# Six similarities and a transposed state sum inside the scan loop of a two-layer decoder kernel

## What is computed

```python
x = _layernorm(x + _L0_attn_ref(x, ...))                 # 1: gated delta rule
x = _layernorm(x + _L0_xattn_ref(x, ctx_1024, ..., 16))  # 2: strided cross attention
x = _layernorm(x + _L0_ffn_ref(x, ...))                  # 3: feed forward with sines
x = _layernorm(x + _L1_attn_ref(x, ...))                 # 4: selective scan
x = _layernorm(x + _L1_xattn_ref(ctx_1024, x, ...))      # 5: attention, 8 heads
x = _layernorm(x + _L1_ffn_ref(x, ...))                  # 6: token-shift mix
```

```python
# 4
def step(h, inp):
    u_t, dt_t, B_t, C_t = inp
    dA = jnp.exp(dt_t[..., None] * A)
    h = h * dA + (dt_t * u_t)[..., None] * B_t[:, None, :]
    y_t = jnp.einsum('bds,bs->bd', h, C_t) + D_param * u_t
    return (h, y_t)
...
y = y * _silu(z)
return y @ W_out + b_out
# 5 (x is the context here, latents the stream; 8 heads)
xn = _layernorm(x, gamma_media, beta_media)
ln = _layernorm(latents, gamma_lat, beta_lat)
...
attn = jax.nn.softmax(sim, axis=-1)
# 6
r = jax.nn.sigmoid(jnp.einsum('btc,dc->btd', xr, W_r))
...
out = r * jnp.einsum('btc,dc->btd', k_act, W_v)
```

## Time and profile before

| | us |
|---|---|
| median of 3 runs | 406.8 (404.0 to 408.42) |
| the profiled execution, its own time | 406.31 |
| its span in the trace | 403.4 |
| mean granted TensorE clock, share of full | 0.954 |
| scan loop, first to last step | 158.0 to 289.8 |
| units of block 5 behind the loop, last `output5` ends | 389.9 |
| end of the span | 403.4 |

### The profile page before, as it was taken

One profiled execution on the slowest core, in us unless ns is written; L12 is line 12 of the kernel. 1 busy time (PEld: TensorE's weight loads), 2 busy tenths in 40 slices (PEclk: granted clock), 3 DMA queues, 4 the chain that ended last, 5 costly groups with the idle time before them and its releaser, 6 DMA issues. The chain is left out here.

```text
span 403.4 us, 5113 instructions
## 1 busy us (share of the span) xinstructions
PE 331.6 (82%) x1578; PEld 221.6 (55%) x1578; DVE 319.8 (79%) x638; ACT 210.8 (52%) x462; POOL 224.4 (56%) x228
## 2 busy tenths in 40 slices
PE   5538748789788889779997888895899999999991
PEld 2332447787564626332433543352498877898870
DVE  1599999996877798999999899799868544754536
ACT  2642222231255669577777165663456666674650
POOL 3599899993413142779899889995502700100002
PEclk9957959999999989999999999999999999999996
DMA  8900000000000003335444434443200000000001
GB/s 267 382 30 0 0 3 1 2 1 2 0 2 0 0 2 107 95 101 160 143 139 138 150 99 126 122 137 103 61 0 1 2 0 2 1 2 2 0 0 52
DMA packets 11520, 24.52 MB, mean 61 GB/s; under 512 B 1231, under 2 KB 2255, under 8 KB 11239
## 3 DMA queue, kind: packets, MB, share of 16 engines
q1 hardware_dynamic: 11495, 24.22, 19.0%
HBM read 23.63 MB, written 0.59 MB: 60 GB/s over the span
## 5 line engine op out<-in xcount | busy, mean ns | idle before, releaser
L1057 POOL TENSOR_TENSOR arena<-arena 128x512 f32<-128x512 f32 x63 | 79.7, 1278 | 24.7 <-DVE arena L685 23.2
L685 DVE TENSOR_TENSOR_SCAN arena<-arena,ps 128x512 f32<-128x512 f32 x64 | 77.2, 1208 | 0.0
L1736 PE MATMUL ps<-arena,first_in 128*128 128x512 f32 x128 | 66.5, 603 | 5.7 <-POOL arena L1057 5.6
L1349 ACT ACTIVATE arena<-ps,arena 128x248 f32<-128x248 f32 x64 | 29.3, 463 | 41.4 <-DVE arena L716 41.4
L678 DVE TENSOR_TENSOR ps<-arena,ps 128x512 f32<-128x512 f32 x64 | 43.4, 680 | 6.0 <-PE ps L1724 5.4
L1313 ACT ACTIVATE arena<-arena,neg_a 128x508 f32<-128x508 f32 x64 | 43.2, 709 | 9.5 <-DVE arena L685 8.6
L1103 POOL TENSOR_TENSOR rstd<-veps,mhalf 128x4 f32<-128x4 f32 (+2 forms) x6 | 5.2, 860 | 74.4 <-DVE veps L782 68.3
L1570 PE MATMUL ps<-arena,first_in 128*128 128x128 f32 (+1 forms) x256 | 31.7, 286 | 12.8 <-POOL arena L916 12.8
L1570 PEld LDWEIGHTS ps<-arena,first_in 128*128 128x128 f32 x256 | 30.7, 201 | 14.1 <-issue 8.1
L1724 PE MATMUL ps<-arena,pick_wide 96*128 96x512 bf16 x64 | 24.5, 385 | 12.9 <-DVE arena L685 12.8
L1736 PEld LDWEIGHTS ps<-arena,first_in 128*128 128x128 f32 x128 | 23.3, 191 | 20.7 <-POOL arena L1057 12.8
(11 more groups left out here) (285 smaller groups left out, 815.4 us busy)
## 6 DMA issues: line engine op xcount, KB each, us to landing
arena<-c_rows_dram SPq DMA_DIRECT2D x64, 256.0 KB, 3.2
fold_in<-in_fold_dram SPq DMA_DIRECT2D x1, 2056.0 KB, 15.0
late_in<-in_late_dram SPq DMA_DIRECT2D x1, 1422.5 KB, 18.4
early_in<-in_early_dram SPq DMA_DIRECT2D x1, 921.5 KB, 9.3
xres<-in_x_dram SPq DMA_DIRECT2D x1, 512.0 KB, 6.2
rows_in<-in_rows_dram SPq DMA_DIRECT2D x1, 512.0 KB, 15.9
kv_ctx<-in_context_dram SPq DMA_DIRECT2D x1, 480.0 KB, 11.0
first_in<-in_first_dram SPq DMA_DIRECT2D x1, 465.0 KB, 3.8
```

Of the source, the lines that this page charges most:

```text
L685: nc.vector.tensor_tensor_scan(hist[:, q % NBUF], fade[:, q % NFADE], chain(q), 0.0, ALU.mult, ALU.add).then_inc(S("scan"), 1)
L1057: tt(seen[:, q % NBUF], hist[:, q % NBUF], c_wide[:, q % NBUF], ALU.mult).then_inc(S("read_out"), 1)
L1349: act(s5_p[:, u % 2, h], sim_bank(u)[:, h * 256:h * 256 + KV], ACT.Exp, bias=s5_max[:, u % 2, h:h + 1], accum_out=s5_den[:, u % 2, h:h + 1 ...
L1736: mm(y_bank, ident, seen[:, p % NBUF], start=False, stop=p % NS == NS - 1).then_inc(S("seen_used"), 1)
```

## The change

1. **Sums in alternate banks.** `y_bank(m)` for the sum m (0 to 3) is bank 0 for even and 5 for odd m, so a new sum no longer waits until the last one is taken out.
2. **Second half transposed.** `accumulate` of steps 32 to 63 issues four turns of 128 columns each that add into the bank, instead of one matmul of 512 columns; the sum comes out transposed. `skip_term` follows with four matmuls. ACT copies the sum (`y_out`), PE turns it back (`turn_back`, four turns), and DVE gates it from PSUM (`gate_turned`).
3. **Block 5 earlier.** Queries start one loop step earlier; similarities 0 to 5, turns 0 to 3 and mixes 0 and 1 are inside the loop. Behind it k runs from 4, `similar` goes two units ahead, and the s5_z buffer is 4 deep. The queries of the second half of the batches go two per k, for four k.
4. **Context norm** moves out of the loop's front and second half: statistics on DVE and a square root on ACT in block 1, the scaling on ACT there, and the turns, with gamma and beta applied in the transposed form on ACT and turned back on PE, at steps 28 to 33. POOL's two large operations (`media`) and its small power are gone.
5. **Block 6**: `Tanh` in place of `Sigmoid`, with `(1 + tanh) / 2` folded into the two DVE operations; part 0's `gated_residual`, `variances6`, `finish6` are inside the loop over k; parts 1 and 2 follow closely on each other.
6. Two input DMAs (context, fold) are issued ahead of two others (early, x); `stay_awake` in the second half issues two matmuls per step in place of one, for five steps.

```diff
+        def y_bank(m):
+            return bank(5 if m % 2 else 0)
+        def y_back(m):
+            return bank(0 if m == 2 else 6)
...
-            return bank(4 + u % 2)
+            return bank(4 if u == 0 or u % 2 else 0)
... accumulate
-                mm(y_bank, ident, seen[:, p % NBUF], start=False, stop=p % NS == NS - 1).then_inc(S("seen_used"), 1)
+                last = p % NS == NS - 1
+                if p < NK4:
+                    ins = mm(y_bank(p // NS), ident, seen[:, p % NBUF], start=False, stop=last)
+                else:
+                    for b in range(HB):
+                        ins = mm(y_bank(p // NS)[:, b * T:(b + 1) * T], seen[:, p % NBUF, b * T:(b + 1) * T], ident,
+                                 is_transpose=True, start=False, stop=last and b == HB - 1)
+                ins.then_inc(S("seen_used"), 1)
+            def turn_back(m):
+                pe.wait_ge(S("y0_out"), m)
+                for b in range(HB):
+                    ins = turn(y_back(m)[:, b * T:(b + 1) * T], yg[:, m % 2, (HB + b) * T:(HB + b + 1) * T], ident)
+                ins.then_inc(S("y_back"), 1)
... PE's loop
-                        m = p // NS
-                        if m % 2:
-                            pe.wait_ge(S("y0_out"), m // 2 + 1)
-                        elif m:
-                            pe.wait_ge(S("y_gated"), NH)
-                        skip_term(m % 2, m // 2)
+                        skip_term(p // NS % NH, p // NK4)
...
-                    stay_awake(1, 7)
+                    stay_awake(2, 6)
...
+                if q == NK4 + 13:
                     similar(0)
+                if q == NK4 + 16:
+                    similar(1)
+                if q == NK4 + 17:
+                    turn_probabilities(0)
+                if q == NK4 + 19:
+                    turn_back(2)
+                if q == NK4 + 21:
+                    pe.wait_ge(S("y_gated"), NH + 1)
+                    similar(2)
+                if q == NK4 + 22:
+                    turn_probabilities(1)
                 if q == NK4 + 25:
-                    similar(1)
-                if q == NK4 + 28:
-                    turn_probabilities(0)
-                    similar(2)
+                    similar(3)
+                if q == NK4 + 26:
+                    mix_context(0)
+                if q == NK4 + 27:
+                    turn_probabilities(2)
+                    similar(4)
+                if q == NK4 + 29:
+                    mix_context(1)
+                    turn_probabilities(3)
                 if q == NK4 + 30:
-                    turn_probabilities(1)
+                    similar(5)
... DVE's loop
-                if q == NK4 + 22:
-                    gate_first(1)
+                if q == NK4 + 20:
+                    gate_turned(2)
... ACT, part 6
-                act(gate6[...], bank(turned6[part])[...], ACT.Sigmoid).then_inc(S("recept"), 1)
+                act(gate6[...], bank(turned6[part])[...], ACT.Tanh, scale=0.5).then_inc(S("recept"), 1)
... DVE behind the loop
-            for part in range(len(PARTS)):
-                gated_residual(part)
-                variances6(part)
-                if part:
-                    finish6(part - 1)
-            finish6(part)
+            gated_residual(1)
+            gated_residual(2)
+            variances6(1)
+            variances6(2)
+            finish6(1)
+            finish6(2)
```

More of the change, by code:

```diff
@@ L425, in _ @@
                 nc.vector.tensor_copy(qkvt[:, :, b], bank(b)[:, 0:3 * D + 2 * H].rearrange("p (n h) -> p n h", h=H)).then_inc(S("qkv_odd"), 1)
+                if b == B - 3:
+                    ve.wait_ge(S("ctx_in"), 16)
+                    for i in range(2):
+                        step(nc.vector.bn_stats(cstats[0:TC, i], kv_ctx[0:TC, i]))
+            for b in range(2, B):
+                step(nc.vector.bn_stats(cstats[0:TC, b], kv_ctx[0:TC, b]))
+            join()
+            for b in range(B):
+                step(nc.vector.bn_aggr(cmv[0:TC, b], cstats[0:TC, b]))
+            join()
+            ts(cveps[0:TC], cmv[0:TC, :, 1], EPS, None, ALU.add).then_inc(S("ctx_var"), 1)
             for n in range(2):
@@ L635, in _ @@
             rectified(3)
-            ve.wait_ge(S("ctx_in"), 16)
-            for b in range(B):
-                step(nc.vector.bn_stats(cstats[0:TC, b], kv_ctx[0:TC, b]))
-            join()
-            for b in range(B):
-                step(nc.vector.bn_aggr(cmv[0:TC, b], cstats[0:TC, b]))
-            join()
-            ts(cveps[0:TC], cmv[0:TC, :, 1], EPS, None, ALU.add).then_inc(S("ctx_var"), 1)
             def b_left(g):
@@ L792, in gated_residual @@
                 ve.wait_ge(S("kv_mm"), last)
-                then(tt(gate6[:, h], gate6[:, h], bank(key6[part])[:, 0:(last - first) * T], ALU.mult))
-                then(tt(xrow[:, 0, first:last], xrow[:, 1, first:last],
-                        gate6[:, h].rearrange("p (b c) -> p b c", c=D), ALU.add))
+                then(stt(gate6[:, h], gate6[:, h], 1.0, bank(key6[part])[:, 0:(last - first) * T], ALU.add, ALU.mult))
+                then(stt(xrow[:, 0, first:last], gate6[:, h].rearrange("p (b c) -> p b c", c=D), 0.5,
+                         xrow[:, 1, first:last], ALU.mult, ALU.add))
             def variances6(part):
@@ L803, in finish6 @@
                 norm_finish(6, part, range(*PARTS[part]), xrow[:, 0], xrow[:, 0])
[L805 removed]
+            shift(EARLY + 1)
+            for k in range(EARLY, NU):
                 normal5(k)
[L807 to L812 removed]
+                if k + 2 < NU:
+                    shift(k + 2)
                 if k == 5:
+                    gate_turned(3)
+                if k == 6:
+                    add_residual(4, 1, bank(7))
+                if k == 7:
                     variances(1)
[L815 removed]
+                if k == 8:
                     normal4(1)
[L817 removed]
+                if k == 9:
                     latents(1)
@@ L1145, in _ @@
                 act(fold_qk[:, 4 * g:4 * g + 4], bank(6 + g).rearrange("p (h c) -> p h c", h=4), ACT.Copy).then_inc(S("fold_qk"), 1)
+            ac.wait_ge(S("ctx_rstd"), 1)
+            for b in range(B):
+                act(kv_ctx[0:TC, b], kv_ctx[0:TC, b], ACT.Identity, bias=cmean_rstd[0:TC, b:b + 1],
+                    scale=crstd[0:TC, b:b + 1]).then_inc(S("ctx_norm"), 1)
             ac.wait_ge(S("late_in"), 16)
@@ L1478, in square6, with tanh6 @@
                 act(kg, kg, ACT.Square).then_inc(S("k_act"), 1)
-            def sigmoid6(part):
+            def tanh6(part):
                 first, last = PARTS[part]
                 ac.wait_ge(S("r6_mm"), last)
-                act(gate6[:, first * T:last * T], bank(turned6[part])[:, 0:(last - first) * T], ACT.Sigmoid).then_inc(S("recept"), 1)
-            for k in range(2, NU + 2):
-                if k == 9:
+                act(gate6[:, first * T:last * T], bank(turned6[part])[:, 0:(last - first) * T], ACT.Tanh,
+                    scale=0.5).then_inc(S("recept"), 1)
+            y_out(3)
+            for k in range(EARLY, NU + 2):
+                if k == 11:
                     latents_out(1)
@@ L1926, in _ @@
             pe.wait_ge(S("scan"), NQ)
-            for k in range(2, NU + 3):
-                if k + 1 < NU:
-                    similar(k + 1)
-                if k == 3:
-                    output4(1, 6, range(HB))
-                if k >= 3:
-                    output5(k - 3)
+            mixed = 0
+            for k in range(EARLY, NU + 3):
+                if k + 2 < NU:
+                    similar(k + 2)
+                if k >= 6:
+                    while mixed <= k - 3:
+                        output5(mixed)
+                        mixed += 1
                 if k < NU + 2:
```

335 lines of the change are left out of this document (190 added, 145 removed).

## The result

| | us |
|---|---|
| before, median of 4 executions beside it | 406.1 (404.0 to 408.4) |
| changed, median of 4 | 393.6 |
| ratio | 0.973, 95% interval 0.968 to 0.978 |
| span of the profiled execution, before and after | 403.4 and 391.2 |
| forecast | 391.5, range 388.5 to 400 |

What follows compares the result with a forecast made beforehand. DVE was taken to bound the scan loop, PE the stretch behind it, and DVE the end. Terms 0.35 - 7.1 - 5.5 - 1.4 - 2.0 = -15.65 us gave 391.2 from 406.8; forecast 391.5, range 388.5 to 400.

Steps and rivals of the forecast that it cites:

- the likeliest case: Whole kernel: the forecast 391.5 us holds within its own range, 388.5 to 395; chance 0.62.
- the waits behind the loop: Behind the loop: with `similar` two units ahead, PE waits less; -1.4 us, bounds -2.4 and +1.5.
- Block 1, +0.35: Block 1 and the loop's front: a small reciprocal and product between two normalizations on DVE's chain add 0.35 us.
- The loop, -7.1: Scan loop's second half: query-step waits -4.3, change of halves -1.2, gate -2.9, extra `shift`s and `inverse5` +1.3; -7.1 us.
- -4.3 in the query steps: Loop's second half: cheaper transposed sums give PE room, so DVE's waits in steps with queries go; -4.3 us.
- -2.9 for the gate: Loop's second half: `gate_first` with two SBUF inputs (3.5) gives way to `gate_turned` reading PSUM (0.6); -2.9 us.
- the bank: Change of halves: with alternate banks the new sum's opening no longer waits for the gate; 1.2 us saved.
- Units moved, -5.5: PE's stretch behind the loop: similarities, turns and mixes moved into the loop and cheaper last sums save 5.5 us.
- The end, -2.0: Kernel's end: part 0's product, statistics and normalization leave DVE's last chain; -2.0 us, bounds 0 and -4.0.
- Rival 1: Loop: handshakes of units 0 to 5 block PE and DVE; 5 to 7 us come back, 397 to 399; chance 0.16.
- Rival 2: Loop: accumulating turns cost like the matmul, 0.85 per step, making PE the bound; 397 to 398; chance 0.06.
- Rival 3: Loop's second half: PE's clock falls, up to 1.7 us each; thirteen falls give about 413; chance of that many 0.05.

Runs made afterwards that it cites:

- The profiled execution without the filler: Changed kernel with the five pairs of matmuls that nobody reads (`stay_awake`, steps 4 to 8 of the second half) left out; 394.0 us.
- the base: The changed kernel run again, unedited, as the comparison for the edits; 393.8 us, span 391.6.

## Why the prediction was right, and where it was not

The time is 2.1 us above the forecast, inside its own range, and the likeliest case is the one that came. Part of that closeness is luck: the forecast started from 406.8, and the kernel before took 406.1 beside this measurement. The saving is 12.5 us where 15.3 was forecast, and nearly all that is missing is one term, the waits behind the loop. Point by point:

- **Block 1, +0.35: not to be told.** DVE's chain is 0.27 us later at 23 us, close to the forecast, and 0.03 at 100.87, where DVE has just waited 1.32 for PE; the first scan starts at 159.14 and before at 159.16. I carried a delay over 130 us in which the profile shows such waits. But the twelve traces that have the changed front unedited and their clock full from 109 to 119 us start their first scan between 158.4 and 160.0, so a term of this size can't be read from one pair. No run undoes the moved context norm or the order of the DMAs.
- **The loop, -7.1: -6.8.** The distances of the scans give it in the prediction's own parts: -4.3 in the query steps, -0.9 at the change of halves, -2.9 for the gate, +1.3 for `shift` and `inverse5`. Only the bank was mis-sized: 1.2 was forecast, the rows give 0.9 and the run with one bank 0.8. The projection ended near 231.2, as reckoned, but DVE waited 0.48 for it and the scan of step 37 came at 232.81 and not at 232.4. The cause given for the -4.3 was only part of it: the waits went by the turns and the spreading of the queries together, and the working gave the spreading no price. Of the 4.1 us that both edits give, only 1.7 hang on the turns once the queries are spread, and half of that is not in the query steps. The gate (-2.9) is as forecast because it compares with a row of that execution, which at 406.31 us is no outlier among the four (404.0 to 408.4); why the operation took 3.57 there stays open, and a SBUF source would cost 0.3 to 0.8 in the new place. The `shift`s came at 0.58, as priced.
- **Units moved, -5.5: held** as far as it was tested, by the one similarity moved back (0.9 for 0.84) and by what is left when the counted waits are taken off. Turns and mixes were not moved back.
- **Waits behind the loop, -1.4: +2.0.** This is the term that failed. Taken period by period, from `mix_context` to `mix_context`, with each matmul at the median of its line, the excess over the period's own work was 3.2 us before (1.2 of it at the wait of the earlier trace rows, which did go) and is 5.2 now, 2.8 of it at the three k with two queries. That is the 2.0 missing between -5.5 and -3.5. I counted ACT's busy share, 61.5 of 100, and took room for order: the pair of `query_out` stood behind a wait in ACT's queue. Moving it ahead brings the excess to 2.1, which is 1.1 less than before and near the -1.4 that I had forecast. The bound of +1.5 that I put on this term was passed.
- **The end, -2.0: -1.9**, and -1.7 by undoing it.
- **Rival 1** did not come: PE's waits for ACT and POOL in the loop are each 0.9 us or less, and the widenings reach DVE in time. Its mechanism, an in-order engine that holds up another, did come behind the loop, where I had not looked for it. **Rival 2** is refuted by the turns' 0.44. **Rival 3** did not come in the changed kernel; the falls that came in edits of it cost the scans of the second half 0 and 0.2 us.

## What to carry to other kernels

Room on an engine and the order in its queue are two things: before pricing a wait at nothing because an engine is half idle, write down what stands ahead of the awaited instruction in its queue and what that waits for. Two edits that make room in the same stretch don't add up, so price each with the other in place. And before filling an idle gap, look which instruction waits: the filler must stand ahead of that one.

## What was not expected of the hardware

- A product of DVE with both inputs in SBUF beside POOL took 0.66 + 0.3 and 0.66 + 0.8 us; each time it ended 0.55 after the POOL operation in which it had started, whose successor took 0.45 longer. The 3.57 us of the earlier trace rows is three operations long. By the Trainium skill (SBUF — State Buffer, SBUF: two separate sides) the lock is held for one instruction; the two runs and the 0.81 of the first half agree, the 3.57 does not, and what is different there stays open.
- The profiled execution without the filler took 398.6 us, its three others 393.7 to 394.0. Its first scan starts at 163.8 us, in the base at 159.6, long before anything that was edited. The clock stood at half for 10.2 us there, where it is full in the changed kernel:

```profile
109.20:119.40 10.20, 8.55 (x29) 6.28 (x29) 5.51 (x11) 1.93 (x4) 1.27 (x1) 0.50 0.00 0
```

```profile
109.20:119.40 10.20, 8.13 (x51) 5.75 (x49) 7.50 (x13) 5.86 (x11) 1.68 (x4) 1.00 0.01 2
```

The first is that execution, the second the changed kernel. The single executions of other kernels that stand 4.3 to 5.5 us above their others have a mean granted clock of 0.943 or 0.944 where the others have 0.955 and more, about what 10 us more at half clock make of 395. Only this one was profiled, so that they have the same cause is likely and not shown.
